# A Mamba-type mixer and gated FFN on one core: second-half angle and factor tables built between the tile steps, and W_out centred on TensorE

## What is computed

```python
x = x + _layernorm(_L0_attn_ref(_layernorm(x), ...))     # mixer
x = x + _layernorm(_L0_ffn_ref(_layernorm(x), ...))      # FFN
# mixer, per token: proj = x @ W_in -> z, x_raw, B (2 x 64), C (64), dt_raw (32), lam_raw (32), theta (32)
dt  = clip(softplus(dt_raw + dt_bias), 1e-4, 0.5); lam = sigmoid(lam_raw)
ang = -cumsum(mean(dt, axis=-1) * theta)                 # along the sequence
C, B = rope(rms(C) * C_bias, ang), rope(rms(B) * B_bias, ang)
# every head: state S_t = exp(dt*A) S_{t-1} + lam*dt * B_t x_t + (1-lam)*dt*exp(dt*A) * B_{t-1} x_{t-1};  y_t = C_t S_t
out = rms(y * silu(z)) @ W_out
# FFN: sigmoid(xr @ W_r.T) * (relu(xk @ W_k.T)**2 @ W_v.T), xr and xk mixed with the previous token
```

## Time and profile before

| what | value |
|---|---|
| median of 3 runs | 256.66 us (256.44 to 256.72) |
| the profiled execution's own time | 257.01 us |
| its span in the trace | 255.2 us |
| PE busy | 223.2 us, 87% |
| DVE busy | 210.0 us, 82% |
| ACT busy | 188.1 us, 74% |
| POOL busy | 162.8 us, 64% |

### The profile page before, as it was taken

One profiled execution on the slowest core, in us unless ns is written; L12 is line 12 of the kernel. 1 busy time (PEld: TensorE's weight loads), 2 busy tenths in 40 slices (PEclk: granted clock), 3 DMA queues, 4 the chain that ended last, 5 costly groups with the idle time before them and its releaser, 6 DMA issues.

```text
span 255.2 us, 6621 instructions
## 1 busy us (share of the span) xinstructions
PE 223.2 (87%) x1962; PEld 174.8 (68%) x1962; DVE 210.0 (82%) x646; ACT 188.1 (74%) x724; POOL 162.8 (64%) x279
## 2 busy tenths in 40 slices
PE   0895899688999998999999999999999999997930
PEld 0893444467788777868878886887688868755930
DVE  1779999987688987975998999889899987975762
ACT  2356748769987789876887797799769976977742
POOL 7433125666789698685868686867586775567351
PEclk9999689999999999999999999999999999999995
DMA  5980000000000000000000001000100100011023
GB/s 121 222 267 0 3 0 0 1 0 4 3 3 3 0 3 1 3 0 5 4 0 3 0 5 41 3 0 11 35 4 0 45 0 3 0 42 37 8 57 77
DMA packets 10199, 6.45 MB, mean 25 GB/s; under 512 B 864, under 2 KB 9856, under 8 KB 10160
## 3 DMA queue, kind: packets, MB, share of 16 engines
q1 hardware_dynamic: 10016, 5.77, 9.5%
q0 software_dynamic: 144, 0.21, 0.4%
HBM read 3.88 MB, written 2.10 MB: 23 GB/s over the span
## 4 chain that ended last, share of the span: by engine, by line
PE 48%; ACT 18%; issue 12%; DVE 11%; POOL 7%; DMA 2%; ACTq 1%; DVEq 0%; POOLq 0%
PE bank L979 9%; PE bank L1060 5%; PE bank L973 5%; PE pair L967 5%; PE bank L881 5%; ACT dt_all L747 4%; ACT bt L686 3%; PE bank L848 3%; PE bank L1120 2%; PE bank L1119 2%; ACT bank L675 2%; ACT junk L664 2%; PE bank L1096 2%; PE bank L1099 2%; DMA w_sb<-w_in 2%
## 5 line engine op out<-in xcount | busy, mean ns | idle before, releaser
L675 ACT ACTIVATE bank<-bank,rsn 128x512 f32<-128x512 f32 x32 | 21.1, 661 | 20.9 <-PE bank L881 20.8
L1377 DVE TENSOR_TENSOR x<-bank,wx 128x512 f32<-128x512 f32 x32 | 21.9, 684 | 16.6 <-ACT bank L675 13.6
L979 PE MATMUL bank<-x,sg 64*64 64x256 f32 x256 | 34.6, 385 | 0.0
L979 PE MATMUL bank<-xg,sg 64*64 64x256 f32 x256 | 33.8, 376 | 0.0
L967 PE MATMUL pair<-x,turned_bc 64*64 64x256 f32 x224 | 29.6, 376 | 0.0
L547 POOL TENSOR_TENSOR y<-ysum,zs 128x256 f32<-128x256 f32 x32 | 23.5, 734 | 6.3 <-DVE ysum L1400 6.2
L973 PE MATMUL bank<-st,bt 64*64 64x256 f32 x128 | 20.8, 395 | 5.9 <-ACT bt L686 5.0
L455 POOL TENSOR_TENSOR rb<-mse,halfn 128x2 f32<-128x2 f32 x32 | 23.5, 735 | 2.5
L452 POOL TENSOR_TENSOR mse<-msb,eps_all 128x2 f32<-128x2 f32 x32 | 8.0, 250 | 26.1 <-ACT junk L666 26.0
L979 PEld LDWEIGHTS bank<-xg,sg 64*64 64x64 f32 x256 | 21.4, 133 | 4.8
L427 POOL TENSOR_TENSOR x_lo<-xnT_all,x_hi 128x128 fp32r<-128x128 f32 x32 | 14.7, 460 | 14.8 <-ACT x_hi L590 14.8
(11 more groups left out here) (195 smaller groups left out, 763.4 us busy)
## 6 DMA issues: line engine op xcount, KB each, us to landing
x_all<-x SPq DMA_DIRECT2D x16, 128.0 KB, 4.3
out<-o_all SPq DMA_DIRECT2D x14, 128.0 KB, 2.5
cm<-consts SPq DMA_DIRECT2D x1, 640.0 KB, 5.4
w_sb<-w_in SPq DMA_DIRECT2D x1, 480.0 KB, 4.4
out<-o_all SPq DMA_DIRECT2D x4, 64.0 KB, 2.2
cm<-consts POOLq DMA_DIRECT2D x1, 128.0 KB, 4.2
wo_sb<-w_out SPq DMA_DIRECT2D x1, 128.0 KB, 4.8
bcb_sb<-bc_bias SPq DMA_DIRECT2D x1, 96.0 KB, 3.8
```

The source lines that it names most:

```text
L675: nc.scalar.activation(x_ps[:], x_ps[:], ACT.Silu, scale=rsn[:, par:par + 1]).then_inc(S["x_silu"], 1)
L979: mm = nc.tensor.matmul(y_ps[half(h)], sg[half(h), a, r], rx(x, r)[half(h)], start=start, stop=stop)
L1377: vec.tensor_tensor((x1, xg)[a][:, par].rearrange("p (a e) -> p a e", e=P), x_ps[:].rearrange("p (a e) -> p a e", e=P), wx[:, par, a].unsq ...
```

## The change

Second-half work moves from the head into the tile steps:

- PE: `angle_sums(1)` stands behind step 1, `next_factors(1)` behind step 3; both use bank 7.
- DVE: `thetas(1)` behind step 0, `whole_turns(1)` behind step 1, `sine_cosine_angles(1)` behind step 2, `mixing_weights` behind step 3, `token_weights(1)` behind step 4.
- ACT: `cos_sin` of the second half in steps 4 to 6 instead of 1 to 3; DVE's wait for it stands ahead of step 12 instead of step 4. POOL's wait for the second half's weights moves from step 4 to step 8.

W_out arrives transposed (`.T` on the host), into `wo_t`. Two products on PE with the matrix `centring` (identity less 1/128) turn it back and take the mean out, into bank 3; one ACT copy behind its step -1 brings it to `wo_sb`. DVE's reduction, and POOL's scaling and two subtractions, are gone.

```diff
-            pool.wait_ge(s_wo, 1)
-            nc.gpsimd.tensor_scalar(wo_mean[:], wo_mean[:], 1.0 / D, None, ALU.mult).then_inc(s_wo, 1)
...
-                elif 0 < n < NQ:
-                    cos_sin(1, slice(NT // 2, NT), ((0, 1), (2,), (3,))[n - 1])
+                elif NQ <= n < NQ + 3:
+                    cos_sin(1, slice(NT // 2, NT), ((0, 1), (2,), (3,))[n - NQ])
+                if n == -1:
+                    act.wait_ge(s_wo, 1)
+                    nc.scalar.activation(wo_sb[:].rearrange("p k n -> p (k n)"), bank[3][:, 0:DI], ACT.Copy)\
+                        .then_inc(s_wo, 1)
...
             next_factors(0)
-            angle_sums(1)
-            next_factors(1)
+            pe.wait_ge(s_w2, 16 * 6)
+            for k in range(2):
+                mm = nc.tensor.matmul(bank[3][:, k * D:k * D + D], wo_t[:, k * 128:k * 128 + 128], c_("centring"), start=True,
+                                      stop=True)
+            mm.then_inc(s_wo, 1)
...
                 for n in range(-1, NT):
                     step(n, general)
+                    if n == (0 if general else 1):
+                        angle_sums(1)
+                    if n == 3:
+                        next_factors(1)
...
-            thetas(1)
-            dve.wait_ge(s_w2, 16 * 6)
-            vec.tensor_reduce(wo_mean[:], wo_sb[:], AX_X, ALU.add).then_inc(s_wo, 1)
...
                 step(-2, NQ - 2, general)
+                step(-1, NQ - 1, general)
+                step(0, 0, general)
+                thetas(1)
+                step(1, 1, general)
                 whole_turns(1)
-                step(-1, NQ - 1, general)
-                token_weights(1)
-                step(0, 0, general)
-                sine_cosine_angles(1)
-                step(1, 1, general)
                 dve.wait_ge(s2, CS_HALF)
                 step(2, 2, general)
+                sine_cosine_angles(1)
+                step(3, 3, general)
                 mixing_weights()
-                step(3, 3, general)
-                dve.wait_ge(s2, TABLES_AT)
-                for n in range(NQ, NT):
+                step(4, 0, general)
+                token_weights(1)
+                for n in range(NQ + 1, NT):
+                    if n == 3 * NQ:
+                        dve.wait_ge(s2, TABLES_AT)
                     step(n, n % NQ, general)
```

More of the change, by code:

```diff
@@ L190, in build @@
         TURN_BANKS, SCALAR_BANKS, W_BANKS = (0, 1, 4, 5), (2, 3, 7), (6, 0)
-        CUM_BANKS, DECAY_BANKS, ANGLE_BANKS, NEXT_BANKS = (6, 7), (2, 5), (4, 3), (6, 7)
+        CUM_BANKS, DECAY_BANKS, ANGLE_BANKS, NEXT_BANKS = (6, 7), (2, 5), (4, 7), (6, 7)
         s2 = sem("tables_scalar")
@@ L284, in build @@
         fnb = sb("fnb", 128, 4 * NQ)
-        wo_mean = sb("wo_mean", 128, 2)
+        wo_t = sb("wo_t", 128, DI)
         xn2 = flat(dt_all).rearrange("p (q d) -> p q d", d=D)
@@ L386, in _ @@
             sp_.dma_start(cm[:, 2:], consts[:, 256:].rearrange("p (n m) -> p n m", m=128)).then_inc(s_c2, 16)
-            for dst, src in ((wo_sb[:], w_out.rearrange("(k p) n -> p k n", p=128)), (wr_sb[:], w_r), (wk_sb[:], w_k),
+            for dst, src in ((wo_t[:], w_out), (wr_sb[:], w_r), (wk_sb[:], w_k),
                              (wv_sb[:], w_v), (mu_sb[:], mu), (bcb_sb[:], bc_bias.partition_broadcast(128))):
@@ L564, in tiles @@
                 for n in range(-2, NT - 1):
-                    if n == NQ:
+                    if n == 2 * NQ:
                         pool.wait_ge(S["weights"], 4)
@@ L923, in next_factors @@
                     pe.wait_ge(t_b[1], 1)
+                    pe.wait_ge(t_turn[1], 3)
                 pe.wait_ge(s2, S_CUM[j])
@@ L988, in mix @@
                     pe.wait_ge(S["st_zero"], 2)
-                    pe.wait_ge(t_turn[1], 3)
                 pe.wait_ge(S["t_sb"], min(n + 2, NT))
@@ L1037, in mix_general @@
                 if i == 0:
-                    pe.wait_ge(t_turn[1], 3)
+                    pe.wait_ge(s_wo, 2)
                 pe.wait_ge(S["yt_sb"], i)
@@ L1049, in y_turn @@
                 pe.wait_ge(S["o_sb"], i)
+                if i == 0:
+                    pe.wait_ge(s_wo, 2)
                 for k in range(2):
@@ L1056, in y_out @@
                 pe.wait_ge(S["yt_sb"], i + 1)
-                if i == 0:
-                    pe.wait_ge(s_wo, 4)
                 for k in range(2):
@@ L1573, in step @@
                     rotations(n + 2, (q + 2) % NQ)
+            dve.wait_ge(s_w2, 16 * 6)
             biased(0)
@@ L1619 @@
         "bc_bias": np.concatenate([bb, cb, bb]),
-        "w_out": np.asarray(L0_attn_W_out),
+        "w_out": np.asarray(L0_attn_W_out).T,
         "w_r": np.asarray(L0_ffn_W_r).T,
```

## The result

| | before | after |
|---|---|---|
| median, 6 runs each | 256.57 us (255.78 to 257.24) | 261.46 us (259.73 to 263.06) |
| ratio after to before, 95% interval | | 1.0192 (1.0156 to 1.0228) |
| profiled execution, span | 257.01 us, 255.2 us | 259.73 us, 257.9 us |

Slower by 4.9 us, against +5.2 us forecast. The six times after lie in two groups, 259.7 to 260.1 and 262.8 to 263.1, and the profiled execution is of the lower one. So the trace has to be read with care before the forecast is called exact. The median itself, 261.46, lies between the groups, where no run was.

A forecast was written before the change was run, and what follows sets the result against it. Neither PE nor DVE alone bounds it; PE's loop takes 4.83 us per step, DVE's 4.02. -1.4 (head) +2.5 (steps 0, 1) +3.8 (steps 2 to 4) +0.3 (ACT) = +5.2 us: median 261.9 us, uncertainty 260.3 to 263.6.

The forecast's parts named there:

- the gain in the head: Head up to x(2): with second-half work removed, x(2) starts at 50.53, a gain of 1.39 us.
- `thetas(1)` ahead of ysum(0): DVE behind step 0: its 2.62 us put ysum(0) at 52.86, against 53.45 before.
- the 2.0 us wait for `angle_sums(1)`: Step 2: DVE idles 2.0 us ahead of whole_turns(1) until PE's sums are complete at about 58.85.
- `next_factors(1)`: PE ahead of x(5): its 2.37 us come first, so x(5) starts at 72.86 against 67.95.
- the ACT copy of 0.28 us: ACT, head: copying W_out adds about 0.28 us to the path from squares(1) to bt(1).
- `mixing_weights`: DVE behind step 3: at most 1.66 us, covered by next_factors(1), costs nothing; uncovered up to 0.9 us.
- token_weights(0) needs the last product of next_factors(0), started at 39.41, so it starts at about 40.5: DVE, head: it starts at about 40.5 instead of 41.54, a gain of 1.04 us.
- A fall after the first costs nothing on the path: PE's clock falling after about 2 us idle ahead of turn(0) is free, as PE waits for thetas(1) anyway.
- rival (1): PE's clock falls ahead of mix(1) or mix(2): 1.5 to 4 us more, 264.2 us likeliest; chance 0.15.
- the new holes would be worse than their own length: PE idle about 2 us ahead of turn(0) and y_turn(0), 1.7 ahead of y_turn(1): throttling adds to their length.
- (2): Tile steps: DVE's insertions hide and only PE's work counts, +2.7 us, 259.3 us; chance 0.10.
- (3): Tile steps: PE's work too falls into its waits, 2.5 us faster, 254.1 us; chance 0.08.

The follow-up runs named there:

- warm_both: Changed kernel with two unused 512-column PE products ahead of turn(0) and two more ahead of y_turn(0); 259.89 us, 1.0145 of before.
- next_head: Changed kernel with next_factors(1) back behind next_factors(0) on PE and token_weights(1) behind step -1 on DVE; 260.01 us, 1.0161 of before.
- next_head_warm: next_head with two unused products of 512 columns on PE ahead of y_turn(0); 258.14 us, 1.0092 of before.
- thetas_head_warm: thetas_head with five unused products of 512 columns on PE ahead of turn(0); 260.07 us, 1.0146 of before.
- before_again: The kernel before, run once more unedited for a second trace; 255.39 us in one run.
- warm_head: Changed kernel with two unused products of 512 columns on PE ahead of turn(0); 261.53 us, 1.0203 of before.
- best2: best with DVE's second-half work cut into pieces spread over the steps and ACT taking one sine table per step in steps 3 to 6; 253.59 us, 0.9894 of before.
- best: Changed kernel with thetas(1) and next_factors(1) back in the head, and angle_sums(1), whole_turns(1), sine_cosine_angles(1) and token_weights(1) moved earlier; 256.64 us, 1.0017 of before.
- thetas_head: Changed kernel with thetas(1) back in DVE's head behind biased(0) and angle_sums(1) on PE behind step 0; 261.30 us, 1.0189 of before.

## Why the prediction was right, step by step

**The path through the steps was right, nearly to the tenth.** The forecast was built on the head of before's trace, with 6.8 us of PE at 1.2 GHz, and assumed no further fall. warm_both's trace, of the changed kernel with four products added, has just that head and no further fall, and differs from the forecast by 0.15 us at x(1), 0.12 at x(2), 0.08 at x(4), 0.11 at x(6) and 0.02 at x(7). This covers the gain in the head of 1.4 us at x(2), `thetas(1)` ahead of ysum(0), the 2.0 us wait for `angle_sums(1)`, whose row in after is 2.02, the sines' 1.66 us, and `next_factors(1)`. warm_both's execution took 262.69 us, where 262.2 was forecast against 257.0: 0.16 us of it is a later w_lo, 0.3 us come at x(29). One step of the working does not hold as written: DVE's start of `thetas(1)` was put 1.55 us earlier, as 1.67 less what the ACT copy of 0.28 us holds back, which would be 1.39. It was 1.71 us earlier from w_lo (25.66 against 27.37), so the copy held back nothing there.

**The parts.** next_head and next_head_warm show `next_factors(1)` on the path with 2.2 us of its 2.37 between x(4) and x(6), and with 1.7 us in the medians. thetas_head_warm shows `thetas(1)` and the wait ahead of whole_turns(1) together with 2.8 us between x(1) and x(4). `mixing_weights`, bounded by 1.66 us, takes 0.99 (before, 62.31 to 63.30).

**What the prediction didn't see.** The step "token_weights(0) needs the last product of next_factors(0), started at 39.41, so it starts at about 40.5" took a start from a trace in which PE had run at 1.2 GHz for 6.8 us. With 3.4 us it starts at 37.34, which is 14.16 us behind w_lo where the forecast had 16.1. In the kernel before this made no difference behind w_lo, as before_again shows. The change, by clearing DVE's head, makes PE's head the bound, and so makes the time depend on the clock by 3.1 us instead of 1.4. Like with like, the change costs 259.8 - 255.4 = 4.4 us with the short stretch and about 262.9 - 257.0 = 5.9 us with the long one. That the median of the first six comes out at +4.9 is luck: three runs fell into each group, and their middle lies where no run was. The second six have their median at 259.81, +3.5 us and below the 260.3 that the prediction gave as its lower end of uncertainty. The sum of 5.2 is 0.5 us below warm_both's 5.7 for the long stretch, and 0.8 us above the 4.4 of the short one, to which eight of the twelve runs belong by their times.

**The clock.** "A fall after the first costs nothing on the path" was right: after has that fall, 6.8 us of it, and its x(4) fits the path without it once the 1.7 us of the head are taken off (40.39 less 1.7 is 38.7; 38.90 measured). The sign that the prediction gave for rival (1), a granted clock under 1 between 42 and 62 us, was too wide, for this harmless fall met it too. Rival (1) itself, a fall at mix(1), did not show in the changed kernel's traces, but it is real: warm_head and next_head have it, and it cost 1.5 to 1.7 us, the low end of the 1.5 to 4 given. The Trainium skill's rule (TensorE: Matmul & The Clock Gate, Part 1: The HAM clock gate), that idle time throttles the array, agrees with these traces: the granted clock fell to 0.50 at 41.5 us in after, behind a hole of 1.87 us ahead of turn(0) at 39.54, and stayed at 1.00 from 38 to 58 us in warm_both, where the holes were filled. That the new holes would be worse than their own length was true of one and not of the other: the same fall cost nothing ahead of mix(0) and 1.5 to 1.7 us at mix(1).

**The other rivals.** (2), that DVE's insertions hide, was false for insertions of 1.7 to 2.6 us and true for those of up to 1.0 us in best2. (3), that all the moved work falls into waits, was false for this order; best2 has a median of 253.6, where (3) had 254.1, with the work in other places.

## What to carry to other kernels

Where two engines feed each other in a loop, measure each engine's slack per round and insert work in pieces of about that length: the same 8 us of table building on DVE cost 1.6 to 1.9% in pieces of 1.0 to 2.6 us and gave -1.1% in the median in pieces of 0.6 to 1.8 us. The two kernels also differ in where PE does its part, so this is not the pieces' worth alone; best, with PE's part in the same places as best2 and whole pieces, took 1.0017 of before. Put a producer on one engine ahead of, not behind, the round after which the other engine asks for it. Clearing one engine's head makes another's the bound, so look whether that one's times are stable before they become the path. Where times fall into two groups, forecast and compare group by group; a median between them is no execution's time.

## What the runs showed of the hardware that was not expected

- Work added to PE changed where its clock fell. Two extra products ahead of turn(0) moved the fall from 41.5 us, where it was hidden, to 51.3 us, where it cost 1.7 us (259.8 to 261.5). Two more, ahead of y_turn(0), gave that back (259.9).
- In the head PE was granted 1.2 GHz for 3.4 us or for 6.8 us, for the same program: two lengths and none between, in 14 traces. The long one goes with a later end of PE's slow rows ahead of `w_lo`: turns of 1.06 us per four last until 13 us instead of 11 (before against after), and move `w_lo` by 1.2 us.
- DVE's idle time at the flag's load and branch ahead of token_weights(0) was 0.17 to 0.19 us behind `biased(0)`, and 0.78 us behind `thetas(1)` in three traces, with its inputs there since 37.1 us (thetas_head). That the load and branch of the queue were covered by `biased(0)` in the one case and not in the other is my reading; it was not tried apart.
